# Cross-attention layer on one core: K and V projected two batches ahead instead of three, the maxima split after their transposition, single groups for the products with V at the end

## The reference

```
Q = x @ Wq.T + bq;  K = ctx @ Wk.T + bk;  V = ctx @ Wv.T + bv      # x (8,112,256), ctx (8,375,256)
attn = softmax(Q_h K_h.T / 4)                                       # per head, 16 heads of 16
o = concat_h(attn V_h) @ Wo.T + bo + x
out = layernorm(o) * gamma + beta                                   # over the 256 features
```

## Time and profile before

| | before |
|---|---|
| median of 3 runs | 156.24 us (154.76 to 158.16) |
| the profiled execution's own time | 157.02 us |
| its span in the profile | 155.2 us |
| busy in the span: PE / DVE / ACT / POOL | 134.0 / 105.6 / 80.4 / 60.7 us |
| granted TensorE clock, mean of the span | 0.982 |

### The profile page before, as it was taken

One profiled execution on the slowest core, in us unless ns is written; L12 is line 12 of the kernel. 1 busy time (PEld: TensorE's weight loads), 2 busy tenths in 40 slices (PEclk: granted clock), 3 DMA queues, 4 the chain that ended last, 5 costly groups with the idle time before them and its releaser, 6 DMA issues.

```text
span 155.2 us, 3853 instructions
## 1 busy us (share of the span) xinstructions
PE 134.0 (86%) x1466; PEld 116.7 (75%) x1466; DVE 105.6 (68%) x247; ACT 80.4 (52%) x163; POOL 60.7 (39%) x83
## 2 busy tenths in 40 slices
PE   5799989679979999889998998999899996779850
PEld 4599779468768899769988987899787875667620
DVE  6745997757937769947896699578779887031252
ACT  3648437214426666526655666465656565566410
POOL 8946997920003998404140504130023023041051
PEclk9999999987999999999999999999999999999997
DMA  4976989698950250697414050405031001001002
GB/s 128 358 259 216 269 296 227 159 270 239 301 204 2 102 156 0 169 267 235 135 52 151 4 178 4 155 2 183 24 128 34 4 4 30 4 4 30 4 0 59
DMA packets 14354, 19.58 MB, mean 126 GB/s; under 512 B 2192, under 2 KB 13520, under 8 KB 14336
## 3 DMA queue, kind: packets, MB, share of 16 engines
q1 hardware_dynamic: 13056, 17.26, 35.6%
q0 software_dynamic: 592, 1.70, 4.5%
q10 hardware_dynamic: 688, 0.38, 0.8%
HBM read 6.30 MB, written 0.92 MB: 47 GB/s over the span
## 4 chain that ended last, share of the span: by engine, by line
PE 65%; DVE 11%; DMA 10%; ACT 6%; issue 5%; SPq 1%; POOLq 0%; ACTq 0%; DVEq 0%
PE m_bank L793 19%; PE pv_bank L873 12%; PE st_bank L857 11%; PE mx_bank L834 10%; DMA q_stack<-shift 6%; DVE mx L656 6%; PE m_bank L901 4%; DMA c_raw<-ctxT 3%; PE m_bank L884 2%; ACT pw L561 2%; PE st_bank L793 2%; DMA q_stack<-q_first 1%; DVE q_hl L618 1%; PE m_bank L841 1%; ACT o_normT L552 1%
## 5 line engine op out<-in xcount | busy, mean ns | idle before, releaser
L656 DVE TENSOR_REDUCE mx<-mx_bank 112x1 f32<-112x375 f32 x128 | 64.6, 541 | 20.4 <-PE mx_bank L834 19.8
L561 ACT ACTIVATE pw<-st_bank 125x448 f32<-125x448 f32 x90 | 48.5, 548 | 48.5 <-PE st_bank L857 47.7
L834 PE MATMUL mx_bank<-k_stack,q_stack 128*112 128x376 f32 x128 | 41.3, 351 | 2.2 <-DVE mx L656 1.2
L857 PE MATMUL st_bank<-q_stack,k_stack 128*125 128x224 f32 x180 | 37.7, 294 | 1.7 <-DMA q_stack<-shift 1.7
L857 PEld LDWEIGHTS st_bank<-q_stack,k_stack 128*125 128x125 f32 x180 | 30.0, 190 | 5.5 <-issue 3.0
L834 PEld LDWEIGHTS mx_bank<-k_stack,q_stack 128*112 128x112 f32 x128 | 22.0, 181 | 4.5 <-DVE mx L656 2.4
L359 POOL TENSOR_TENSOR c_hl<-c_raw,c_hl 128x752 fp32r<-128x752 f32 x6 | 10.9, 1814 | 27.5 <-DVE c_hl L612 27.5
L873 PE MATMUL pv_bank<-pw,v_sb 125*17 125x112 f32 x720 | 20.4, 260 | 1.1 <-ACT o_raw L535 1.1
L405 POOL TENSOR_SCALAR var_eps<-mv 112x1 f32<-112x1 f32 x7 | 1.6, 223 | 49.2 <-DVE mv L692 49.2
L793 PE MATMUL m_bank<-c_hl,w_hl 128*128 128x376 f32 x84 | 18.7, 365 | 0.9 <-ACT w_hl L449 0.9
L873 PEld LDWEIGHTS pv_bank<-pw,v_sb 125*17 125x17 f32 x720 | 16.3, 97 | 3.9 <-issue 2.2
(11 more groups left out here) (102 smaller groups left out, 160.6 us busy)
## 6 DMA issues: line engine op xcount, KB each, us to landing
k_stack<-k_hl SPq DMA_DIRECT2D x48, 188.0 KB, 2.5
c_raw<-ctxT SPq DMA_DIRECT2D x8, 375.0 KB, 4.3
q_stack<-q_hl SPq DMA_DIRECT2D x6, 224.0 KB, 4.5
q_stack<-q_hl SPq DMA_DIRECT2D x6, 168.0 KB, 3.4
x_space<-x_nat POOLq DMA_DIRECT2D x1, 896.0 KB, 10.3
out<-yo SPq DMA_DIRECT2D x8, 112.0 KB, 1.9
pw<-wT SPq DMA_DIRECT2D x2, 256.0 KB, 4.8
x_space<-xT SPq DMA_DIRECT2D x1, 448.0 KB, 6.1
```

Source lines behind the costliest of these rows:

```text
L561: nc.scalar.activation(p_tile[0:KC, n % PR, :, :], st_of(n)[0:KC, 0:4 * Q].rearrange("p (j q) -> p j q", j=4), ACT.Exp, scale=float(DK) ** ...
L656: nc.vector.tensor_reduce(mx[b % 2][:, h % 2, q_pair(h // 2):q_pair(h // 2) + 1], mx_bank[n % MR][0:Q, 0:KV], axis=AX_X, op=ALU.max, negat ...
L834: nc.tensor.matmul(mx_bank[n % MR][0:Q, 0:KVP], q_stack[k][:, side, q_pair(h // 2), b - Q_STACKS[k][0], :], k_stack[b % 3][:, h // 2, :], ...
L857: last = nc.tensor.matmul(st_of(n)[0:KC, k * 2 * Q:(k + 1) * 2 * Q], k_stack[i % 3][:, 2 * g + k, c * KC:(c + 1) * KC], q_stack[qk][:, :, ...
```

## The change

- K and V of batch i + 2 are projected in batch i (AHEAD = 2), so their last projections are in batch 5 instead of batch 4. From batch 1 on the halves of K are at u = 3 and 5, the parts of V at u = 9, 10 and 11. K and V of batch 2 leave the prologue and go into batch 0.
- A half of K of batches 2 to 7 is taken in other steps: ACT copies it from PSUM into `k_full` with its bias, then ACT rounds it into the high part, then GpSimd subtracts to make the low part (`take_k`, `subtract_k`). The three DMAs stay. The high part of the context moves from DVE to ACT, the scaling of the layer norm from DVE to GpSimd.
- The maxima go unsplit through PE; DVE splits them as it takes them out of PSUM (`split_shift`). `stack_shift` is now two DMAs on SP's queue, behind the six of `stack_k` and ahead of the store. For batch 0 the maxima go in two halves of eight heads, through ACT's queue.
- The prologue has 14 heads instead of 20; the heads per unit and the places of the other jobs change. MT stands at u = 8 (u = 10 in batch 0). The ONT of an earlier batch goes into the same bank with MT, and OUT comes three batches after its batch instead of one.
- Q is projected in four stacks (batches 0; 1 and 2; 3 to 5; 6 and 7) instead of three.
- From the fourth unit of batch 6 on, `values` runs one group at a time (in batch 7 it did so before).

The core of the diff:

```
-AHEAD = 3
+AHEAD = 2
-Q_STACKS = ((0, 1), (1, 1 + GB), (1 + GB, B))
+Q_STACKS = ((0, 1), (1, 3), (3, 6), (6, B))
-U_K = (0, 2)
-U_V = (3, 5, 8)
-U_OT, U_ONT, U_OUT = 5, 9, 11
-HEADS = (1, 1, 2, 1, 2, 1, 1, 1, 2, 1, 2, 1)
-EARLY_HEADS = H + 4
+U_OUT, U_OT, U_BIAS, U_Q = 2, 6, 1, 1
+U_K = ((4, 6), (3, 5))
+U_V = ((9, 10, 11), (10, 11, 9))
+NORM_WITH = {3: 0, 4: 1, 5: 2, 6: 3, 7: 5}
+U_MT = (10, 8, 8, 8, 8, 8, 8)
+EARLY_HEADS = 14
+HEADS = (2, 2, 2, 1, 2, 1, 2, 1, 1, 1, 1, 0)
+FIRST_HEADS = ((2, 1, 2, 2, 2, 2, 2, 2, 2, 2, 2, 1),)
...
+            def take_k(b, t):
+
+                src = wait_full(act, "K", b, t)
+                if b > AHEAD:
+                    act.wait_ge(k_lo, 2 * (b - 1) + t + 1)
+                nc.scalar.activation(k_full[:, t, :], src[:, 0:KVP], ACT.Identity,
+                                     bias=bqk[:, 2 + t:3 + t]).then_inc(k_taken, 1)
+                act.wait_ge(k_taken, 2 * (b - AHEAD) + t + 1)
+                act.wait_ge(k_in[(b - 2) % 3][t], 48 * ((b - 2) // 3 + 1))
+                nc.scalar.copy(k_hl[b % 2][:, 0, t, :], k_full[:, t, :]).then_inc(k_hi, 1)
...
+            def subtract_k(b, t):
+
+                pool.wait_ge(k_hi, 2 * b + t + 1)
+                nc.gpsimd.tensor_tensor(k_hl[b % 2][:, 1, t, :], k_full[:, t, :], k_hl[b % 2][:, 0, t, :].bitcast(F32),
+                                        op=ALU.subtract).then_inc(k_lo, 1)
...
+            def split_shift(src, to, n):
+
+                nc.vector.tensor_copy(to[:, 0, :], src).then_inc(shift_hi, 1)
+                dve.wait_ge(shift_hi, n)
+                nc.vector.tensor_tensor(to[:, 1, :], src, to[:, 0, :].bitcast(F32), op=ALU.subtract).then_inc(shift_ready, 1)
...
+            def stack_shift(b):
+
+                k = q_stack_of(b)
+                to = q_stack[k][:, :, :, b - Q_STACKS[k][0], :].rearrange("p s a q -> p (s a) q")
+                sp.wait_ge(shift_ready, b + 2)
+                for part in range(2):
+                    row = SPREAD * (part + 1) - 1
+                    sp.dma_start(to[row:row + 1, :, :].bitcast(F32),
+                                 shift[b % 2][:, part, :].bitcast(F32)).then_inc(shift_in[b % 2], 16)
...
+                if i + AHEAD < B:
+                    for t in range(2):
+                        stack_k(i + AHEAD, t)
+                if i + 1 < B:
+                    stack_shift(i + 1)
...
-                    elif u % (2 * NC) == 1 + late and n > 2 and not (i == B - 1 and u > 2):
+                    elif n >= SINGLE and u % NC == 1 + (n > WIDE) and not (i == B - 1 and u > 2):
+                        values(*divmod(n // NC - 1, NG))
+                    elif n < SINGLE and u % HALF == 1 and n > 2:
                         for group in (n // NC - 2, n // NC - 1):
                             values(*divmod(group, NG))
```

More of the change, by code:

```diff
@@ L38 @@
 UNITS = NG * NC
-GB = 4
+GB = 3
 VW = DK + 1
@@ L74 @@
[L74 to L79, removed]
+U_OUT, U_OT, U_BIAS, U_Q = 2, 6, 1, 1
+U_K = ((4, 6), (3, 5))
+U_V = ((9, 10, 11), (10, 11, 9))
+HALF = UNITS // 2
+NORM_WITH = {3: 0, 4: 1, 5: 2, 6: 3, 7: 5}
+U_MT = (10, 8, 8, 8, 8, 8, 8)
@@ new lines @@
+EARLY_HEADS = 14
+EARLY_JOBS = {1: ("Q", 1, 0), 3: ("Q", 1, 1), 5: ("V", 1, 0), 7: ("V", 1, 1), 9: ("MT", 0, 0), 10: ("V", 1, 2)}
+FIRST_JOBS = {1: (("MT", 0, 1),), 7: (("Q", 2, 0),), 8: (("Q", 2, 1),)}
+S0_JOBS = [("Q", 0, 0), ("K", 1, 0), ("V", 1, 0), ("MT", 0, 0)]
+S1_JOBS = [("Q", 0, 1), ("K", 1, 1), ("V", 1, 1)]
+M0_JOBS = [("K", 0, 0), ("V", 0, 0), ("Q", 1, 0)]
+M1_JOBS = [("K", 0, 1), ("V", 0, 1), ("Q", 1, 1), ("MT", 0, 1)]
+for _i in range(B - AHEAD):
+    if _i == 1:
+        M1_JOBS.append(("BIAS",))
+    if _i in (2, 3):
+        M0_JOBS.append(("Q", 3, _i - 2))
+    if _i >= 3:
+        M1_JOBS.append(("OUT", _i - 3))
+    M0_JOBS.append(("K", _i + AHEAD, 0))
+    M1_JOBS.append(("K", _i + AHEAD, 1))
@@ L80 @@
     if _i == 0:
-        M1_JOBS += [("BIAS",), ("Q", 2, 0)]
+        M0_JOBS.append(("Q", 2, 0))
+        M1_JOBS.append(("Q", 2, 1))
     if _i >= 1:
         M1_JOBS.append(("OT", _i - 1))
[L84 to L91, removed]
+    (M1_JOBS if _i == 0 else M0_JOBS).append(("MT", _i + 1))
@@ L100 @@
     _h = MAX_HEADS[-1].stop if MAX_HEADS else EARLY_HEADS
-    MAX_HEADS.append(range(_h, min(B * H, _h + (FIRST_HEADS[_n] if _n < len(FIRST_HEADS) else HEADS[_n % UNITS]))))
+    _i, _u = divmod(_n, UNITS)
+    MAX_HEADS.append(range(_h, min(B * H, _h + (FIRST_HEADS[_i] if _i < len(FIRST_HEADS) else HEADS)[_u])))
 assert MAX_HEADS[-1].stop == B * H
@@ L171, in build @@
         shift_in = [sem(f"shift_in{i}") for i in range(2)]
+        half_in = [sem(f"half_in{t}") for t in range(2)]
         stored = [sem(f"stored{i}") for i in range(2)]
@@ L252, in stack_q @@
             queue.wait_ge(q_lo, 2 * k + 2)
-            queue.wait_ge(q_clear[k], 2 if k == 1 else 1)
+            queue.wait_ge(q_clear[k], 1)
             for slot, part in enumerate((0, 0, 1)):
@@ L289, in _ @@
             load_x(2)
+            load_x(3)
             load_context(2)
@@ L507, in _, with stack_shift_half @@
                 q_hi_part(1, t)
[L508 to L525, removed]
+            v_part(1, 0)
+            for k in range(2, NQ):
+                x_hi_part(k)
+            def stack_shift_half(t):
+                act.wait_ge(shift_ready, t + 1)
+                to = q_stack[0][:, :, :, 0, :].rearrange("p s a q -> p (s a) q")
+                for part in range(2):
+                    row = SPREAD * (part + 1) - 1
+                    act.dma_start(to[row:row + 1, t:2 * NP:2, :].bitcast(F32),
+                                  shift_half[t][:, part, :].bitcast(F32)).then_inc(half_in[t], 16)
+            stack_shift_half(0)
+            v_part(1, 1)
             act.wait_ge(w_lo, 2)
@@ L703, in take_bv @@
                 last.then_inc(bv_ready, 1)
-            for n in range(H):
+            for n in range(EARLY_HEADS):
                 head_max(n)
@@ new lines, in _ @@
+                    if u == U_BIAS and i == 1:
+                        bias_rows()
+                    if u == U_OUT and i >= 3:
+                        layer_norm(i - 3 if i < B - 1 else B - 3)
+                    if i + 1 < B and u == U_MT[i]:
+                        take_shift(i + 1)
+                    if u == U_OT and 1 <= i <= 5:
+                        normalise(i - 1)
+                    if u == 4 and i == 6:
+                        normalise(5)
+                    if u == 6 and i == 6:
+                        layer_norm(4)
@@ new lines, in _ @@
+                    if u == U_Q and i in (2, 3):
+                        q_project(3, i - 2)
+                    if u == U_OUT and i >= 3:
+                        out_project(i - 3 if i < B - 1 else B - 3)
+                    if u == U_OT and 1 <= i <= 5:
+                        transpose_o(i - 1)
+                    if u == 3 and i == 6:
+                        transpose_o_norm(4)
+                    if u == 4 and i == 6:
+                        transpose_o(5)
+                    if u == 6 and i == 6:
+                        out_project(4)
@@ L996, in _ @@
                         transpose_half(0)
                         residual()
-                    if u == U_OUT and i >= 1:
-                        out_project(i - 1)
-                    if u in U_V and i + AHEAD < B:
-                        v_project(i + AHEAD, U_V.index(u))
-                    for n in heads[1:]:
-                        scores_for_max(n)
+                    if i + AHEAD < B:
+                        for t in range(2):
+                            if u == U_K[min(i, 1)][t]:
+                                k_project(i + AHEAD, t)
+                        for c in range(NC):
+                            if u == U_V[min(i, 1)][c]:
+                                v_project(i + AHEAD, c)
@@ L1004, in _ @@
+                    for h in heads[1:]:
+                        scores_for_max(h)
             transpose_norm_half(0)
```

312 lines of the change are left out of this document (156 added, 156 removed).

## The result

The changed kernel takes 178.82 us (median of 4 runs, 176.32 to 180.04) against 156.12 us; the ratio is 1.140 with a 95% interval of 1.118 to 1.161. Of each kernel's runs this ratio, like all that follow, compares only the quick ones, within 1.5% of its fastest. Slower, as forecast, but by 22.7 us where the prediction had 8, and outside its range (up to 170). The profiled execution took 179.17 us, near the upper end of its runs, with a span of 177.4.

What follows compares the result with a forecast made beforehand. PE was taken to bound the kernel, so the forecast is about its waits: 157.0 + 3.6 (batch 6 starting later) + 4.2 (clock) + 0.1 = 164.9 us, given as 164 since before's profiled execution was 0.8 above its median; range 154 to 170.

Steps and rivals of the forecast that it cites:

- five waits for K's stack at u = 7: Batches 1 to 5, head 0 of batch i + 2: PE waits 2.5 us in each, 0.7 of it ahead of OT.
- a way of 5.86 us: K's first half from projection through copies, subtraction and DMA to its landed stack: 5.8 us, against 3.3 of PE work.
- start of unit (0, 0): End of the prologue: the first unit needs only eight maxima and starts at 26.7 us, 6.2 earlier.
- batch 0: First batch: 13.9 us of work, 1.7 for low clock, 0.3 of gaps, 1.2 of wait for the shift.
- batches 1 to 5: Middle batches: 84 us at 16.8 each, plus 4.2 for falls of the clock.
- batch 6: 12.3 us instead of 11.9: more heads, OUT and transpositions fit into idle time, a new shift wait of 1.5.
- batch 7 and the end: After batch 6: OUT earlier gives -0.1 us, the same end chain without OUT between -0.2, single groups of products 0.
- The period at full clock: One of batches 1 to 5: 5.4 us to K's first half, 5.8, then 5.3, 0.3 for the shift: 16.8.
- sum of work: PE's pure work in one of batches 1 to 5, without waits: 14.1 us.
- The clock: Falls to half speed after waits in batches 1 to 5: about 1.4 us each, three of five taken, +4.2.
- The stack of K in time: Rival, batches 1 to 5: no wait for K, at most 15.1 us per batch, 152 us in all; chance 0.15.
- a smaller wait: Rival, batches 1 to 5: wait of 1.2 us and the clock holds, 154.2 us, up to 158; chance 0.13.

Runs made afterwards that it cites:

- the first experiment: The changed kernel with only the four heads of batch i + 2 moved to u = 9, 10, 10 and 11 from 7, 8, 9 and 10: 166.55 us, ratio 1.064.

## Why the prediction missed

The direction, the place and the mechanism were right: five waits for K's stack at u = 7, a way of 5.86 us (forecast 5.8), in each of the five 2.2 to 2.8 us of wait and 0.3 ahead of OT (forecast 2.5 together), a loss that one line about the place of the heads more than halves. The size was wrong, because the period of a batch at full clock was summed too short, the falls of the clock were counted too few, and a wait in batch 0 and one in batch 6 were put at nothing. By the prediction's own terms, against the profiled execution (163.1 us of span forecast, 177.4 measured):

| term | forecast | measured |
|---|---|---|
| start of unit (0, 0) | 26.7 | 25.0 |
| batch 0 | 17.1 | 20.6 |
| batches 1 to 5 | 84 + 4.2 for the clock | 96.6 |
| batch 6 | 12.3 | 15.0 |
| batch 7 and the end | 18.8 | 20.3 |

*The period at full clock* is the largest miss: 18.0 us in batch 2, and 89.8 / 5 = 18.0 with the wait filled, against 16.8, so 5.8 us over five batches. In batch 2 the way from the start of the batch to the end of K's first half took 6.3 us, not 5.4: PE waited there for the low part of Q (0.4 us), and I had laid the units end to end without gaps. The part behind the head took 5.8 instead of 5.6. The prediction held the sign of it: its sum of work, 14.1, and OUT's waits, 0.6, make 14.7, where a batch of the kernel before takes 15.0.

*The clock* comes next. "I take three of five" was a guess between two rows, and it stood for batches 1 to 5 alone. In the profile the clock fell in four of the five, and it was still low in batch 1 from batch 0. In batches 1 to 5 the low clock cost 6.8 us, by the kernel with work in the wait, where I had 4.2; a single fall cost 0.7 to 1.6, about what I had (1.4). A second fall in batch 0, from 42.6 us on, 1.5 us behind the wait that was not foreseen, and one in batch 7 behind the wait for the shift were in no case of mine, and the range counted at most five. (In the profile with OUT of batch 4 later alone, whose batch 0 is the same, the stretch after the prologue was 6.8 us long instead and no second came; the batch took 20.5 us as well.) The one in batch 7 is worth 1.1 us: without it batch 7 and the end took 19.2 us in eight of the other profiles.

*Batch 0.* The start was earlier than forecast, since the maxima were there earlier: the split began at 20.9 us instead of 23.2. The batch itself took 3.5 us more than I had. The wait for the constants was missed (2.2 us on the way of K; with a landing of 3.2 us, PE waited 1.8 at 41.1): I had listed what is queued behind SP's waits and not what GpSimd waits for ahead of its loop; a line of the program that had cost nothing before, since nothing urgent stood behind it.

*Batch 6.* The chain of the changed kernel:

```profile
151.87 0.53 DVE mx L701
152.44 0.48 PE mx_bank L909 x2
...
155.24 1.82 DMA q_stack<-shift
157.10 0.69 PE st_bank L909 x4
```

The wait for the shift was forecast (1.5, measured 1.7). Missed was that unit (6, 8) writes to the maxima's bank and waits for the last of them, which OUT of batch 4 and its layer norm now stand ahead of: 1.4 us. And the sum was wrong: PE's work there, 9.35 us and 2.4 more, with a wait of 1.5 makes 13.3 us, not 12.3. PE was busy for 11.8 of 15.0 us.

*The rivals.* The stack of K in time, and a smaller wait, are refuted: each of the five waits was 2.2 us or longer. Work that went from VectorE to GpSimd: the subtraction takes 1.003 us, as the line between GpSimd's own rows had it, 1.65 times DVE's 0.606. The Trainium skill (GPSIMD Engine Reference, Performance versus the Vector engine) has roughly 2; here it is less, and the 0.2 us more per batch that the prediction worked out from it weren't there.

## What to carry to other kernels

Where a producer's result is needed by an engine that works through a list in order, add up the way (copies, semaphores, every DMA issue, landing) and the work listed between, and put the first consumer behind the longer one: one line that moved four heads was worth 12 of 22.7 us. A wait on TensorE is dearer than its length once the clock falls after it: of fifteen waits of 2.2 to 2.8 us in three profiles twelve had a fall, so price nearly all of such waits with one, count those of every batch, and leave the range room for more. When urgent work moves onto a queue, read the waits that already stand there.

## What the runs showed of the hardware

In the changed kernel, with the constants later and with OUT of batch 4 later alone, each profile has five waits for K's stack of 2.2 to 2.8 us in batches 1 to 5; in each, four had a fall of the granted clock before their end or up to 1.5 us behind it, and one (2.2 us in two of the profiles, 2.8 in the third) had none. PE had been busy for 0.95 us of 3.1 (56.0 to 59.1, and 0.96 in 113.1 to 116.2) when the clock fell, for 3.4 us; a double group of products then takes 2.3 instead of 1.27 us. Three waits of 1.4, 1.6 and 2.0 us, with the heads later, had no fall behind them; with K's low part on DVE, where waits of 0.9 and 0.6 us follow each other, it fell once in five batches. Useless matmuls in the wait paid for themselves, 5.1 us in all.

The last DMA of the first half of K landed 2.2 to 2.8 us after its issue in batches 1 to 5 of the changed kernel, and 3.2 to 7.9 us in batch 0 of the kernels with the load of x ahead of it. With that load issued later it took 2.4 us instead of 5.8, in the kernel with K earlier. The same DMA took 3.5 to 4.2 us in three batches of the first experiment; why stays open.
